# Three quarters of a per-position attention moved into the loop of the cross-attention ahead of it

## The reference, cut to what matters

```
x = x + L3_xattn(ctx_1024, layernorm(x))     # layer 9: 16 heads, 257 + 32 keys for each batch
x = x + L3_attn(layernorm(x))                # layer 10
x = x + L3_ffn(layernorm(x))                 # layer 11: attention and experts

def L3_attn(x, w_qkvw, w_out):               # H = 16, HD = 2, four groups
    qkvw = x @ w_qkvw                        # each of 4 groups gives q, k, v and w of 32 features
    ...                                      # the 32 features of a row pair become 16 "positions" x 2
    scores = q @ k^T * HD ** -0.5            # 16 x 16 for each position block
    o = softmax(scores) @ v
    return (o * w) @ w_out
```

## Time and profile before

| | before |
|---|---|
| median of three runs | 2186.41 us |
| profiled execution, its own time | 2167.64 us |
| its span | 2165.7 us |
| loop of layer 9 | 1237 to 1736.5 us of the span |
| layer 10 | 1736.6 to 1932.7 us |
| busy: PE, DVE, ACT, POOL | 84%, 68%, 47%, 34% |
| mean granted TensorE clock | 0.916 |

### The profile page before, as it was taken

One profiled execution on the slowest core, in us unless ns is written; L12 is line 12 of the kernel. 1 busy time (PEld: TensorE's weight loads), 2 busy tenths in 40 slices (PEclk: granted clock), 3 DMA queues, 4 the chain that ended last, 5 costly groups with the idle time before them and its releaser, 6 DMA issues. The chain is left out here.

```text
span 2165.7 us, 50175 instructions
## 1 busy us (share of the span) xinstructions
PE 1808.7 (84%) x20226; PEld 1196.8 (55%) x20226; DVE 1478.9 (68%) x3575; ACT 1013.0 (47%) x2544; POOL 731.6 (34%) x951
## 2 busy tenths in 40 slices
PE   6678999899978789986677799999999987756596
PEld 4324557556645556643556566777677652234386
DVE  6799995688875665557870477665666479987723
ACT  5535664566644722243412356666666422215243
POOL 2244554455541514214431311000000056533543
PEclk9778999999999999998779999999999998867688
DMA  8000000100026100080034201000000000021187
GB/s 343 1 1 0 1 0 1 75 5 5 5 80 277 42 2 1 1 331 2 2 116 128 65 25 37 13 20 20 21 20 1 1 1 10 19 101 71 32 296 239
DMA packets 57670, 130.63 MB, mean 60 GB/s; under 512 B 13961, under 2 KB 36188, under 8 KB 51808
## 3 DMA queue, kind: packets, MB, share of 16 engines
q1 hardware_dynamic: 54144, 121.32, 15.6%
q0 software_dynamic: 3296, 6.12, 0.8%
HBM read 107.97 MB, written 20.12 MB: 59 GB/s over the span
## 5 line engine op out<-in xcount | busy, mean ns | idle before, releaser
L319 POOL TENSOR_TENSOR arena<-arena 128x4 f32<-128x4 f32 (+2 forms) x97 | 113.9, 1176 | 772.9 <-DVE arena L263 336.4
L3293 ACT ACTIVATE arena<-PS,arena 128x289 f32<-128x289 f32 x256 | 127.4, 509 | 107.7 <-DVE arena L3401 107.7
L1870 POOL TENSOR_TENSOR arena<-arena 128x128 f32<-128x128 f32 x384 | 141.2, 409 | 42.8 <-PE PS L1733 20.0
L3401 DVE TENSOR_REDUCE arena<-PS 128x2 f32<-128x578 f32 x128 | 94.0, 755 | 76.3 <-PE PS L3181 76.3
L3181 PE MATMUL PS<-arena 128*128 128x289 f32 x512 | 135.5, 408 | 2.1 <-DVE arena L3395 0.9
L1806 DVE RECIPROCAL arena<-PS 128x128 f32<-128x128 f32 x96 | 91.5, 954 | 48.2 <-PE PS L1771 48.2
L1256 POOL TENSOR_TENSOR arena<-arena 128x512 f32<-128x512 f32 x64 | 84.0, 1313 | 109.9 <-DVE arena L1401 109.9
L1837 ACT COPY arena<-PS 32x128 f32<-32x128 f32 x384 | 99.5, 259 | 44.7 <-PE PS L1747 39.7
L3181 PEld LDWEIGHTS PS<-arena 128*128 128x128 f32 x512 | 92.2, 190 | 24.1 <-issue 2.2
L366 PE MATMUL PS<-arena 128*128 128x512 f32 x176 | 92.5, 658 | 12.4 <-DVEq L4199 11.7
L1852 ACT ACTIVATE arena<-arena 128x512 f32<-128x512 f32 x96 | 60.6, 631 | 65.7 <-DVE arena L1799 63.4
(11 more groups left out here) (419 smaller groups left out, 4774.2 us busy)
## 6 DMA issues: line engine op xcount, KB each, us to landing
arena<-in_ctx SPq DMA_DIRECT2D x32, 1091.0 KB, 10.2
arena<-in_f_w SPq DMA_DIRECT2D x39, 514.0 KB, 5.0
arena<-in_ctx SPq DMA_DIRECT2D x16, 834.0 KB, 14.7
lists<-arena SPq DMA_DIRECT2D x8, 1040.0 KB, 10.8
arena<-in_f_w SPq DMA_DIRECT2D x32, 256.0 KB, 3.1
arena<-in_ctx SPq DMA_DIRECT2D x16, 512.0 KB, 3.7
arena<-in_mid SPq DMA_DIRECT2D x1, 3796.5 KB, 11.9
arena<-in_late SPq DMA_DIRECT2D x1, 3204.0 KB, 10.3
```

The costliest lines, as they stand in the source:

```text
L319: e.tensor_tensor(x, x, half.broadcast_to(list(x.shape)), ALU.pow).then_inc(*T.done("norm_root", tag))
L1870: k = e.tensor_tensor(dst[:, b], spread(src[:, b, :], [P, HG, S], 1), spread(self.g.C["headmask"], [P, HG, S], 2), ALU.mult)
L3293: e.activation(self.weights(n, k, 0, UL), PS[:, k, 0:UL], ACT.Exp, bias=self.st[:, h, k:k + 1], accum_out=self.st[:, h, 4 + k:5 + k]).then ...
L3401: e.tensor_reduce(self.st[:, n % 2, 2 * k:2 * k + 2], PS[:, 2 * k:2 * k + 2, 0:UL], AXX, ALU.max, negate=True).then_inc(*T.done("k3_least" ...
```

## The change

Layer 10 is cut by tiles instead of by groups of features. Quarter q is now tiles 4q to 4q + 3 of the residual stream, with all four groups stacked along the partitions. Quarters 0 to 2 are worked on inside the loop of layer 9, behind the tiles that the loop has finished; quarter 3, and what is left of quarter 2, come after the fence. `self.inner` is layer 10, and `step_pe`, `step_dve`, `step_act` and `step_pool` are called at the end of a loop step.

More of the change, by code:

```diff
@@ L3374, in dve @@
         e.tensor_tensor(x, x, W["x3_b1"][0:NB, :], ALU.add).then_inc(*T.done("x3_last", 0))
-        for i in range(2):
-            self.key_norm(e, T, i)
+        e.memset(self.own("eps"), 1e-5)
+        e.memset(self.own("minus"), -1.0).then_inc(*T.step())
         self.key_gain(e, T, 0)
@@ L3478, in by_four @@
[L3478 to L3502 removed]
+        NP, NU = self.NP, self.NU
@@ new lines, in rest, with unit, store @@
+    def rest(self, table):
+        last = NB + BT - 2 - 16 * (self.LAST - 1) - self.START
+        return [table[d] for d in sorted(table) if d > last]
+    def unit(self, u):
+        return self.NU * (self.LAST - 1) + u
+    def store(self, e, T, q, half=None):
+        t, NP, BG = self.g.t, self.NP, self.BG
+        if half is None:
+            for w in T.due(("m3_mixed", self.NU * q + self.NU - 1)):
+                e.wait_ge(*w)
+        else:
+            for w in T.due(("m3_mixed", ("end", half))):
+                e.wait_ge(*w)
+        lo, hi = (0, 32) if half is None else (16 * half, 16 * half + 16)
+        for c in range(4):
+            for r in range(2):
+                at = 2 * BG * c + BG * r
+                e.dma_start(t["mixed"][c][BG * q:BG * q + BG].rearrange("b (h r f) -> r b h f", h=NP, r=2)[r][:, :, lo:hi],
+                            self.o[at:at + BG, :, lo:hi]).then_inc(*T.done(f"m3_back{q}", (half, "out", c, r), 16))
@@ new lines, in fetch @@
+    def fetch(self, e, T, q, half=None):
+        for w in T.due((f"m3_back{q}", (half, "out", 3, 1))):
+            e.wait_ge(*w)
+        for c in range(4):
+            e.dma_start(self.back[q][:, c, :], self.g.t["mixed"][c][self.BG * q:self.BG * q + self.BG].rearrange(
+                "b (i d) -> (b i) d", d=D)).then_inc(*T.done(f"m3_back{q}", c, 16))
+    def sp(self, e, T):
+        self.store(e, T, 2)
+        self.fetch(e, T, 2)
+        for half in range(self.NE):
+            self.store(e, T, self.LAST, half)
+        self.fetch(e, T, self.LAST, self.NE - 1)
@@ new lines, in pool, with stats_dve @@
+        weighed(0)
+        weighed(1)
+        for q in range(self.LAST):
+            self.after.begin_pool(e, T, q)
+    def stats_dve(self, e, T, t):
+        s, own = self.g.small[:, t, :], self.around.own
+        for w in T.due(("k3_added", t)):
+            e.wait_ge(*w)
+        e.bn_stats(s[:, 0:6], self.g.X[:, t, :]).then_inc(*T.step())
+        for w in T.due(T.prev()):
+            e.wait_ge(*w)
+        e.bn_aggr(s[:, 6:8], s[:, 0:6]).then_inc(*T.step())
+        for w in T.due(T.prev()):
+            e.wait_ge(*w)
+        e.tensor_tensor(s[:, 0:1], own("minus"), s[:, 6:7], ALU.mult).then_inc(*T.step())
+        e.tensor_tensor(s[:, 7:8], own("eps"), s[:, 7:8], ALU.add).then_inc(*T.done("norm_var", ("m3", t)))
@@ L3654, in dve @@
+        self.stats_dve(e, T, NT - 1)
+        mixes, totals, maximas = ([self.unit(u) for u in self.rest(x)] for x in (self.MIX_AT, self.TOTAL_AT, self.MAXIMA_AT))
+        self.total_dve(e, T, totals[0])
+        self.maxima_dve(e, T, maximas[0])
+        features_out(1)
+        features_out(3)
         products(0)
+        for q in range(2):
+            residual(q, q)
         products(1)
+        self.mix_dve(e, T, mixes[0], self.mixed)
         maxima(0)
-        for u in range(self.NU):
-            if u:
-                mix(u - 1)
-            if u + 2 < self.NU:
-                products(u + 2)
-            weigh(u)
-            if u + 1 < self.NU:
-                maxima(u + 1)
@@ L3665, in dve @@
-        mix(self.NU - 1)
-        for c in range(self.CN):
-            x = quarter(g.X, c)
-            for w in T.due(("m3_rows", c)):
-                e.wait_ge(*w)
-            e.tensor_tensor(x, four(PS[:, c, :]), x, ALU.add).then_inc(*T.step())
-            for w in T.due(T.prev()):
-                e.wait_ge(*w)
-            self.after.begin_dve(e, T, c)
-            if c:
-                self.after.begin_rows_dve(e, T, c - 1)
+        self.total_dve(e, T, totals[1])
+        maxima(1)
@@ L3678 @@
+        self.mix_dve(e, T, mixes[1], self.mixed)
+        weigh(0)
+        weigh(1)
+        mix(0)
+        mix(1)
+        for q in range(2, NQ):
+            residual(q, q - 2)
+            self.after.begin_rows_dve(e, T, q - 2)
+        self.after.begin_rows_dve(e, T, NQ - 2)
 class L3Ffn(Layer):
```

616 lines of the change are left out of this document (413 added, 203 removed).

## The result

The changed kernel takes 2162.54 us (median of 4 runs, 2157.7 to 2164.05), the kernel before, measured beside it, 2184.61 (4 runs, 2179.29 to 2187.88). The ratio is 0.9889, 95% interval 0.9869 to 0.9908: 22 us faster, where 16 were forecast. The profiled execution has an own time of 2162.10 and a span of 2160.1, so it stands at its median.

A forecast was written before the change was run, and what follows sets the result against it. It took TensorE to bound layer 9's loop and VectorE layer 10: loop +67, layer 10 -88, end +5, so -16 from 2186.4 to 2170 us. The forecast's own range was 2150 to 2185, over all cases 2132 to 2212.

The forecast's parts named there:

- TensorE's added work: Loop: layer 10's 32-column feature blocks at 0.92 us each, plus transposes, add 10 us.
- The wait behind `project`: Loop, once in four steps: TensorE waits 0.6 for the second weights, 0.35 at the fourth score group; 14 us in all.
- The wait at j = 2: Loop: half the keys' scaling at the end of j = 1 delays the first exponential, 0.65 us 14 times, 9 us.
- VectorE's insertions at j = 2: Loop: layer-10 operations behind the add that waits for project, paid in full by TensorE, 14 us.
- The rest of VectorE's insertions: Loop: seven insertions of 1.17 at j = 3, 8 us, and the tile's own statistics, 2 us.
- start and end: Loop's first and last steps: key statistics ahead of the first normal, 1 us, and a later finish, 3.5; sum 4.5.
- Layer 10: Behind the fence: the stage shrinks from 178 to 89.5 us, giving back 88.
- The end: Last store to layer 11: 4 us more, and 1 for layer 11's first transposes waiting for all four parts.
- A: Rival, loop: VectorE and ScalarE find slack in other steps, so the loop grows by only 30, to 2133 us; chance 0.18.
- B: Rival, loop: the fourth score group stops TensorE 0.95 us in nearly all 64 steps, loop +105, 2208 us; chance 0.23.
- C: Rival, loop: GpSimd sets the pace, its passes waiting for VectorE at 8.4 us; some 45 more, 2215 us; chance 0.06.
- D: Rival, behind the fence: the stage takes 105 us instead of 89.5, total 2186 us; chance 0.13.

The follow-up runs named there:

- e4: The kernel before, nothing of layer 10 moved, with three score banks and the division as a product with a reciprocal in PSUM: 2205.81 us, ratio 1.0096.
- e9: The kernel before with three score banks as in e4, but the division left as tensor_scalar on SBUF: 2185.73 us, ratio 1.0054 to the kernel before.
- e1: The changed kernel with VectorE's inserted layer-10 operations at j = 2 ahead of its wait for project: 2142.93 us, 0.9804 of the kernel before.
- e2: The changed kernel with ScalarE's key scaling whole at j = 2, not split over j = 1 and 2: 2152.12 us, 0.9849 of the kernel before.
- e7: The changed kernel with the edits of e1 and e2, and the next division ahead of VectorE's wait for project: 2114.11 us, 0.9727 of before.
- e10: e7 with VectorE's queue behind the fence reordered (last unit's total and first maxima earlier): 2101.28 us, 0.9654 of the kernel before.
- e3: The changed kernel with the old division (reciprocal into SBUF, four tensor_scalar), three score banks kept: 2264.12 us, 1.0366 of the kernel before.

## Why the prediction was right, and where it was not

The sign, the stages and the sum held: -16 forecast, -22 measured, the time inside the likeliest case's own range. First the time of a step in each run, then term by term, with the runs that isolate them:

| first score to first weighing, us, in steps just ahead of n = 25 | before | e4 | e9 | changed | e1 | e2 | e7 |
|---|---|---|---|---|---|---|---|
| j = 3, behind `project` | 2.82 | 3.88 | 3.65 | 3.77 | 3.77 | 3.77 | 2.83 |
| j = 0 | 2.82 | 3.08 | 2.85 | 3.09 | 3.09 | 3.09 | 3.19 |
| j = 1 | 2.82 | 2.83 | 2.82 | 2.83 | 2.82 | 2.83 | 2.83 |
| j = 2 | 2.82 | 2.83 | 2.83 | 3.46 | 3.45 | 2.82 | 2.82 |

- *TensorE's added work, 10:* 384 instructions took 13.0 us, a block 1.0 to 1.08 where I had 0.92. Taken whole, 13 stands for 10; what part of it hides in a wait was not tried.
- *The wait behind `project`, 14:* the mechanism and its size in that step were right (0.6 and 0.35 forecast, 0.68 and 0.35 in e4, the step 1.06 longer for my 0.95), the sum was mis-sized: the next step, at which I put nothing, loses 0.26 more. Banks and product cost 25.9 us in e4's loop (16.7 and 9.2). Some 4.5 of them lie ahead of the first `project`, 61.3 us into the loop in e4 and 56.7 in the changed kernel, so at most 21 hold there: in the three tiles with a feature block behind `project` the step takes 2.93, without these waits.
- *The wait at j = 2, 9:* 8.0 (e2). Right, mechanism and size: 3.46 for 2.82 is 0.64, I had 0.65.
- *VectorE's insertions at j = 2, 14 of the 24:* 18.1 (e1), 11.8 of waits and 5.9 of slower matmuls behind them. The clock was missing from my sum.
- *The rest of VectorE's insertions, 10, ScalarE's, 5, and start and end, 4.5:* 13 + 21 + 8.0 + 18.1 = 60 of 66.2 leave 6 for what was 19.5. The step that was too large is "at j = 3 the keys' statistics use up the slack; d = 2, 10 and 14 add 1.17 each", seven times. In e1, where these stand as in the change, the mechanism shows at four of the seven places, d = 2 and 10 of quarters 0 and 1: the step behind them (j = 0) takes 4.22 us, not 3.09, so 1.1 each and 4.5 in all for my 8. At d = 14 and at d = 2 of quarter 2 TensorE does not wait. Of ScalarE's exponentials those at d = 4 of quarters 0 and 1 cost 0.95 each as I had it (4.41 for 3.46 at j = 2), but they are in e2's 8.0; those at d = 7 cost 0.18. The first `project` comes as early as before (56.7 us into the loop, 57.0 before), and the loop ends 7.7 us behind the start of the last one where it was 4.3: 3.4 for my 3.5. The tile's own statistics were not isolated, and these parts overlap: they do not add up to 66.2 exactly.
- *Layer 10, -88:* -94.7, the stage 83.1 for 89.5. I had seen the mechanism (a pass that waits for a total behind the first maxima); e10 shows what it costs, 9.4. The difference is the 6.5 us that I had added to the order's own 83 for additions at half clock. They did start slow: the second unit's took 8.8 us (1854.1 to 1862.9) where those of the kernel before took 7.0, which is 1.8 and not 6.5. The products ahead of them were done 44.2 us behind the fence for my 46, and so the order's own 83 came out.
- *The end, +4 and +1:* 3.7 and 1.3.

So 66 for 67 is partly luck: terms too small by 3, 7 and 4 met others that were too large by about as much.

Of the rivals, A (waits hide) needed a growth of 30: the changed kernel is far from it, and only e7, with three edits, comes to 29.1. B needed the fourth group's wait at 0.95 in nearly all 64 steps, 61 us: by the weight loads it comes 41 times, 19.6 us in all, in the changed kernel, and 33 times, 10.8 us, in e4. B is out by its size, not because the wait is absent. C would have needed passes of 8.4 us; in the loop they take 1.9 to 2.9, and GpSimd is busy 64% of the 16 steps, where I had 75. (What my text on C calls "the same of two SBUF inputs" is the turn-taking of the products in the earlier trace rows: it is operations with two SBUF inputs that meet GpSimd, not the weighing with one in PSUM.) D is out with 83.1. What I said of the old division, that it would have been shut out, e3 shows at 102 us: the product costs 9 and the bank it needs 17 in the loop, and with the old division the change would be a loss of 3.7%.

## What to carry to other kernels

When work is put under another engine's loop, its place in each queue matters more than its amount: here it was free ahead of an engine's wait, and behind it the bound engine paid in full, and then again at the lower clock. A wait of TensorE can stand in the row of its weight loads and not in that of its matmuls: look at both, and compare the start times of the same step in two kernels. A wait that one sees in a trace can be the cheaper of two: look at what stands in the other queues behind the instruction before moving it. And where VectorE and GpSimd work side by side, write VectorE's small steps so that they do not meet GpSimd at SBUF: here a `tensor_tensor` with one operand in PSUM in place of a `tensor_scalar` or of two operands in SBUF, even at some cost.

## What the runs showed of the hardware that was not expected

- Behind a wait of 3.10 us of TensorE, in a loop that is otherwise busy, the matmuls from 1548.06 to some 1551 ran at the lower level: a weighing of 1.91 for 1.02; that tile's granted clock is 0.95. Taking such waits away gave 5.9 us of busy time back on top of them (e1). In the loop of before the clock is 1.00 behind the first tile, so none of its rows gave this price.
- A `tensor_scalar` of 4 columns can take 4.70 us, as long as the GpSimd pass beside it, and one of 290 columns up to 3.61 for 0.37.
- TensorE's matmul row can show less than half of what a step waits. Behind `project` it has 0.34 us in e1, while the weight loads wait 0.58 and 0.35 and the step is 0.95 us longer than in e7; in e9 it has 0.23, the weight loads 0.46 and 0.35, and the step is 0.83 longer than before.
- Layer 11 has two levels that no edit here made, 227 to 232 and 240 to 243 us, with 171 to 174 and 163 or 164 GB/s of DMA; they go with the chips of the runs. The granted clock does not tell them apart: it was 0.77 in e4 (240.6 us) and in e10 (230.5).
